# Local attention on one core: the mask band written by four small matrix tiles, and the values' copy placed between the two groups of exponentials

## The chip, the cores and the metric

The kernel runs on one core of a Trainium2 chip. The core has a matrix engine (TensorE, PE in the profile, with its weight loads shown apart as PEld), VectorE (DVE), ScalarE (ACT), GpSimd (POOL) and a queue that starts transfers (SP). Each engine runs its own list of instructions in order, and they meet only at semaphores. The time is the device time of one execution in microseconds (us); lower is better. The execution that was profiled is one execution, and its durations are those of that one.

## The reference

The input is x, 8 sequences of 512 tokens with 128 features. A first layer (clustered attention with an MLP) is computed, and then a stack of two layers with local attention. Only the local attention is touched. Cut to what matters, with 8 heads of 64 features and windows of 64 tokens:

```python
q, k, v = split(shift_token(x) @ wqkv)            # per layer, DEPTH = 2
q, k = rotary_xpos(l2norm(q) * qs, l2norm(k) * ksc)
# the keys of a window are the window before it and itself: 128 keys
sim = einsum('bhwid,bhwjd->bhwij', bq * 8, bk)
mask = (i < j) | (i > j + WINDOW) | (j == -1)     # a band; j == -1 ahead of the first window
attn = softmax(where(mask, -max, sim))
out = einsum('bhwij,bhwjd->bhwid', attn, bv)
```

So every query sees the 65 keys up to itself, which in the 64 by 128 block of a window is a diagonal band. The first window of a sequence sees only the keys of its own window.

## The kernel before

The function `local_layers` computes both layers. A tile is 128 tokens, which are two windows of 64; a layer has 32 tiles, four for each of the 8 sequences, and there are 64 tiles in all. The program is a pipeline by slots: in slot n tile T = n is projected, tile R = n - 2 is turned, tile U = n - 3 gets its scores and exponentials, and tile O = n - 4 is weighed with the values. The order on each engine is the order of the calls in that engine's `slot(n)`; no planner moves anything.

PE does in a slot, in this order: `project` of Q and K (L1360), `prob_turn` of the lower half (L1403), `scores` (L1383 and L1390), `transpose` of Q (L1372), `prob_turn` of the upper half, `project` of V, `transpose` of K, one step for a sequence that has ended, and `weigh` (L1419). That step is one of four, which go round with the tiles: the output product in two halves (L1536, two slots), the mean (L1525) and the squares (L1519). Below, a group of four slots is a round, and its slots are named output 1, output 2, mean and squares by the step that PE does in them.

`scores` first writes the mask into the scores' memory `la_s`. The tile `lw_band` holds 0 where a key is seen and -1e30 elsewhere, for 128 rows, which are the 64 queries of each of two windows; a product with a unit matrix `lw_identb` in bf16 copies it. The two products of 512 columns start the sums of two banks, `place(h)` putting the even heads in the first bank and the odd heads in the second. Then 16 f32 products add queries times keys, each in a corner of the array with 64 rows (one head of a pair) and 64 columns (one window).

There is one `la_s`. DVE takes its row maxima (`maxima`, L1603), multiplies them by the inverse norm to the bias (L1609), ACT takes the exponentials in place (`exps`, L1732, four activations for the even heads, then four for the odd ones), and in the next slot DVE divides by the sums (`share`, L1617 and L1621, by halves). The products of the next tile's band wait for both halves of `share`.

Projections and turned tiles go through two banks, `la_ring`, in turn. A product may write a bank when the one before it in that bank has been read. The bank of V is emptied by ACT in `take_values` (L1774), and the next product in that bank is the projection of Q for the next tile, which waits for `v_made`. On ACT the slot's order is: the raw copies of Q and K (L1743), their squares (L1826), the copy of half of the turned probabilities (L1749), the copy of the turned Q (L1756), `take_values`, the bias wait and the eight exponentials, and the small steps behind them (L1783, L1786, and for ended sequences L1842, L1765, L1766, L1853). SP moves the values to `la_v_back` when `v_made` is reached; they are needed four slots later by `weigh`.

DVE's slot order is: both halves of `share`, the copy out of `la_o` (L1636), four products for the rotation (L1584), maxima and bias, the other half of the turned probabilities (L1629), the copy of the turned K (L1645), norms (L1593, L1597), and one addition or subtraction of 512 columns for an ended sequence (L1713 or L1719). POOL rotates (L1883, L1889), polishes the inverse norms (L1868 to L1874), scales the keys (L1896), and once in four slots makes the shifted input of the next sequence by two copies (L1907, L1909).

Of the kernel before, what the change touches and what calls it, by code (L numbers as in the profile page):

```python
# [19 lines left out]
P = 128  # L20
B, S, D = 8, 512, 128
# [1070 lines left out]
LH, LD, WIN = 8, 64, 64  # L1092
# [15 lines left out]
def local_layers(nc, a, X, XT, C, weights):  # L1108
# [9 lines left out]
    with ExitStack() as ctx:  # L1118
# [3 lines left out]
        def ps(name, shape, dt=F32):  # L1122
            return ctx.enter_context(nc.psum_tensor(tag + name, shape, dt))

        def sem(name):
            return a["semaphores"].enter_context(nc.semaphore(tag + name))

        ident, identb, band = weights["ident"], weights["identb"], weights["band"]
# [34 lines left out]
        s_ps = ps("s", [P, LH, KEYS])  # L1163
# [25 lines left out]
        bias_made = sem("bias_made")  # L1189
        exp_half, exp_made = sem("exp_half"), sem("exp_made")  # L1190
# [29 lines left out]
        def tile_at(n):  # L1220
            for T in range(TILES):
                if slot_of(T) == n:
                    return T
            return None
# [5 lines left out]
        def ffn_at(n):  # L1230
            for f in range(BATCHES):
                if ffn_slot(f) == n:
                    return f
            return None
# [10 lines left out]
        s_flat, pT_flat = s_ps[:].rearrange("p h c -> p (h c)"), pT_ps[:].rearrange("p h c -> p (h c)")  # L1245
# [5 lines left out]
        def ring_index(T, use):  # L1251
            return 5 * (slot_of(T) + 2 * (use in (TURN_Q, TURN_K))) + use
# [7 lines left out]
        def ring_count(T, use):  # L1260

            r = ring_index(T, use)
            return sum(ring_used(x) for x in range(r + 1))
# [7 lines left out]
        def ended(n):  # L1271

            T = tile_at(n)
            return T // TPB if T is not None and T % TPB == TPB - 1 else None

        def place(h):

            return 4 * (h % 2) + h // 2
# [48 lines left out]
        def _(pe):  # L1327
# [48 lines left out]
            def scores(T):  # L1376
                b, t = T // TPB, T % TPB
                pe.wait_ge(qT_made, T + 1)
                pe.wait_ge(kT_made, T + 1)
                if T > 0:  # L1380
                    pe.wait_ge(shared, 2 * T)
                for bank in range(2):
                    nc.tensor.matmul(s_ps[:, 4 * bank:4 * bank + 4, :].rearrange("p h c -> p (h c)"), identb[:],  # L1383
                                     band[:, int(t == 0), :], start=True, stop=False, skip_group_check=True)
                for pair in range(4):
                    for w in range(2):
                        for e in range(2):
                            h = 2 * pair + e
                            key = PAD + t * P - WIN + w * WIN
                            mm = nc.tensor.matmul(s_ps[64 * w:64 * w + 64, place(h), :],  # L1390
                                                  qT[64 * e:64 * e + 64, T % 2, pair, 64 * w:64 * w + 64],
                                                  kT[64 * e:64 * e + 64, b % 2, pair, key:key + KEYS],
                                                  start=False, stop=True, skip_group_check=True)
                mm.then_inc(s_filled, 1)
# [331 lines left out]
        def _(act):  # L1726
# [3 lines left out]
            def exps(T, e):  # L1730
                for h in range(e, LH, 2):
                    ins = nc.scalar.activation(s_ps[:, place(h), :], s_ps[:, place(h), :], ACT.Exp,  # L1732
                                               bias=bias[:, T % 2, h:h + 1], scale=inv[:, T % 4, h:h + 1],
                                               accum_out=sums[:, T % 2, place(h):place(h) + 1])
                return ins
# [9 lines left out]
            def take_low(T):  # L1745
                act.wait_ge(pT_filled, 2 * T + 1)
                if T > 0:
                    act.wait_ge(o_filled, 2 * T)
                nc.scalar.activation(probT[:, 0:4], pT_ps[:, 0:4], ACT.Copy).then_inc(pT_low, 1)  # L1749

            def take_qT(T):
                r = ring_index(T, TURN_Q)
                act.wait_ge(ring_filled, ring_count(T, TURN_Q))
                if T - 1 > 0:
                    act.wait_ge(s_filled, T - 1)
                nc.scalar.activation(qT[:, T % 2].rearrange("p c q -> p (c q)"), ring_ps[:, r % 2, :],  # L1756
                                     ACT.Copy).then_inc(qT_made, 1)
# [31 lines left out]
            def take_gate(f, i):  # L1789
                j, m = NC * f + i, HC[i][1]  # L1790
                act.wait_ge(g_filled, j + 1)
                if j - 1 > 0:
                    act.wait_ge(prod_made, j - 1)
                nc.scalar.activation(gate[0:m, j % 2, :], chunk_banks(j)[0][0:m], ACT.Gelu,
                                     bias=b1[0:m, 1, i:i + 1]).then_inc(gate_made, 1)

            def take_hn(f):
                act.wait_ge(divided, f + 1)
                if f % B == 0:
                    act.wait_ge(ffn_loaded, 16 * FFN_LOADS * (f // B + 1))  # L1800
                if NC * (f - 1) > 0:
                    act.wait_ge(a_filled, NC * (f - 1))
                nc.scalar.activation(hn[:, f % 2, :], batch_at(C, f), ACT.Identity,
                                     scale=ln[:, 0:1], bias=ln[:, 1:2]).then_inc(hn_made, 1)

            def slot(n):
                T, N, R, U, O = (tile_at(n - x) for x in (0, 1, 2, 3, 4))
                f, ahead = ffn_at(n), ffn_at(n + 1)
                if f is not None:
                    if O is not None:  # L1810
                        take_low(O)
                        O = None
                    for i in range(NC):
                        take_gate(f, i)
                        if i == 0 and ahead is not None:
                            take_hn(ahead)
                if f is not None and f == B - 1:
                    nc.scalar.preload_act_table_set("natural_log_exp_and_others")
                if T is not None:
                    take_raw(T, 0)  # L1820
                    take_raw(T, 1)
                if N is not None:
                    act.wait_ge(raw_made, 2 * N + 2)
                    if N > 0:
                        act.wait_ge(sum_made, N)
                    nc.scalar.activation(squares[:], raw[:, N % 2], ACT.Square).then_inc(sq_made, 1)  # L1826
                if O is not None:
                    take_low(O)
                if R is not None:
                    take_qT(R)  # L1830
                if T is not None:
                    take_values(T)
                if U is not None:
                    act.wait_ge(bias_made, U + 1)
                    exps(U, 0).then_inc(exp_half, 1)
                    exps(U, 1).then_inc(exp_made, 1)
                b = ended(n - 6)
                if b is not None:
                    act.wait_ge(c_made, b + 1)
                    if b > 0:  # L1840
                        act.wait_ge(m_filled, m_count(b - 1, SQUARE))
                    nc.scalar.activation(csq[:], batch_at(C, b), ACT.Square).then_inc(csq_made, 1)  # L1842
                if N is not None:
                    inverse_norms(N)
                b = ended(n - 5)
                if b is not None:
                    shift(b)
                b = ended(n - 7)
                if b is not None:
                    act.wait_ge(m_filled, m_count(b, SQUARE))  # L1850
                    if b - 1 > 0:
                        act.wait_ge(dev_inverted, b - 1)
                    nc.scalar.activation(var[:, b % 2], m_ps[:, 0:TPB], ACT.Identity, bias=eps[:]  # L1853
                                         ).then_inc(var_made, 1)
                if ahead is not None and f is None:
                    take_hn(ahead)
# [93 lines left out]
def band_mask():  # L1950

    r, c = np.arange(P)[:, None] % WIN, np.arange(KEYS)[None, :]
    seen = (c >= r) & (c <= r + WIN)
    first = seen & ((np.arange(P)[:, None] >= WIN) | (c >= WIN))
    both = np.where(np.stack([seen, first], 1), 0.0, NEG).astype(np.float32)
    return np.ascontiguousarray(np.tile(both, (1, 1, 4)))

# [17 lines left out]
```

## Time and profile before

| | us |
|---|---|
| median of 3 runs | 1480.23 |
| lowest and highest run | 1479.69 to 1481.54 |
| the profiled execution | 1484.96 |
| span of that execution, first to last instruction | 1483.2 |
| granted TensorE clock, mean | 0.957 of full speed |

The local layers fill the span from about 703 us to its end. The steady part of the first layer runs from about 740 to 990 us and that of the second from about 1121 to 1387 us; between and behind them lie the feed-forward parts, which PE fills. In a timeline row the columns are start, duration, engine, line, operation, and what is written and read with shapes; `xN` stands for N merged instructions, and the bracket at the end is the idle time of the engine before the row with what ended it. Where instructions overlap in their engine's pipeline, a recorded duration is longer than the distance to the next start. In the chain of work that ended last, each row is a piece of that chain with its start and its length.

### The profile page before, as it was taken

What the parts mean: (1) busy time and instruction counts of PE and PEld (TensorE: products, weight loads), DVE (VectorE), ACT (ScalarE), POOL (GpSimd) and SP (SyncE); (2) the same over time, 40 slices, a digit from 0 to 9 for tenths busy, and PEclk for the clock granted to TensorE, in tenths of its full rate; (3) what the DMA queues carried; (4) which work ended last, traced back from release to release, by engine and by line L of the source; (5) the groups of instructions that cost most, each with busy time, mean ns of one, the idle gap of its engine ahead of it and who ended that gap; (6) DMA issues with size and microseconds to landing.
All of it is one profiled execution on the core that took longest, in us unless ns stands there. A gap on an engine that the chain in (4) does not pass through costs nothing.

```text
span 1483.2 us, 27541 instructions
## 1 busy us (share of the span) xinstructions
PE 1283.4 (87%) x9444; PEld 647.8 (44%) x9508; DVE 1096.4 (74%) x1943; ACT 1000.0 (67%) x2313; POOL 822.4 (55%) x1005
## 2 busy tenths in 40 slices
PE   3478999899998978598689999988978999999898
PEld 1112322232222212166256666665435666666654
DVE  5778888888887867123599999985448999998544
ACT  4236667666666666587488899885348898988532
POOL 3666776676666620122687788760047777887100
PEclk9569999999999999899799999999999999999899
DMA  3614333333333320100111111100101111111001
GB/s 102 114 36 77 60 65 62 75 61 62 66 71 61 62 51 1 48 10 2 39 27 27 27 30 30 27 19 12 36 22 41 27 27 30 26 27 27 1 15 43
DMA packets 161118, 60.85 MB, mean 41 GB/s; under 512 B 139690, under 2 KB 152788, under 8 KB 160980
## 3 DMA queue, kind: packets, MB, share of 16 engines
q1 hardware_dynamic: 160980, 59.09, 18.8%
q8 instruction: 77, 1.26, 0.4%
q14 instruction: 61, 0.50, 0.1%
HBM read 8.60 MB, written 2.10 MB: 7 GB/s over the span
## 4 chain that ended last, share of the span: by engine, by line
PE 29%; ACT 10%; DVE 7%; issue 4%; POOL 1%; ACTq 0%; DVEq 0%; POOLq 0%
ACT la_s L1732 8%; PE la_ring L1360 6%; PE la_s L1390 4%; PE la_ring L1372 3%; PE la_pT L1464 3%; DVE la_prob L1621 2%; PE la_pT L1403 2%; PE la_m L1536 2%; PE la_ring L1452 1%; PE la_s L1454 1%; PE la_pT L1454 1%; PE la_s L1452 1%; ACT la_v_own L1774 1%; DVE la_sumsq L1593 1%; PE la_s L1383 1%
## 5 line engine op out<-in xcount | busy, mean ns | idle before, releaser
L618 DVE TENSOR_REDUCE row_max<-max_ps 128x2 f32<-128x1024 f32 x256 | 313.0, 1223 | 70.2 <-PE max_ps L430 68.9
L670 ACT ACTIVATE prob<-scores_ps 128x1024 f32<-128x1024 f32 x256 | 262.2, 1024 | 147.5 <-PE scores_ps L410 144.0
L1732 ACT ACTIVATE la_s<-la_s,la_bias,la_inv 128x128 f32<-128x128 f32 x512 | 223.5, 442 | 8.4 <-DVE la_bias L1609 8.4
L1883 POOL TENSOR_TENSOR la_turned<-la_raw,lw_rot 128x1024 f32<-128x1024 f32 x64 | 150.9, 2358 | 127.5 <-PE la_ring L1372 83.7
L1360 PE MATMUL la_ring<-lw_wqkv,la_hT 128*128 128x512 f32 x384 | 200.6, 633 | 15.5 <-DVE la_swapped L1584 6.9
L410 PE MATMUL scores_ps<-stack 128*128 128x512 f16 x512 | 155.5, 386 | 42.0 <-ACT prob L670 41.1
L1889 POOL TENSOR_TENSOR la_turned<-la_turned,la_swapped 128x1024 f32<-128x1024 f32 x64 | 150.7, 2355 | 5.0
L444 PE MATMUL heads_ps<-prob,v_pad 128*32 128x512 f32 x1024 | 137.2, 608 | 1.1 <-ACT prob L670 1.1
L430 PE MATMUL max_ps<-stack 24*128 24x512 f16 x512 | 102.5, 397 | 31.0 <-DVE row_max L618 18.6
L410 PEld LDWEIGHTS scores_ps<-stack 128*128 128x128 f16 x512 | 34.2, 97 | 208.7 <-ACT prob L670 161.6
L1584 DVE TENSOR_TENSOR la_swapped<-la_ring,lw_rot 128x256 f32<-128x256 f32 x256 | 90.9, 416 | 32.2 <-ACT la_raw L1743 22.7
L1732 ACT ACTIVATION_READ_ACCUMULATOR la_s<-la_s,la_bias,la_inv 128x1 f32 x512 | 111.0, 217 | 0.0
L776 POOL TENSOR_TENSOR cl<-cl,cl_inv 128x512 f32<-128x512 f32 x60 | 63.0, 1050 | 85.0 <-DVE cl_inv L559 85.0
L1360 PEld LDWEIGHTS la_ring<-lw_wqkv,la_hT 128*128 128x128 f32 x384 | 64.5, 194 | 63.3 <-issue 40.0
L1621 DVE TENSOR_TENSOR la_prob<-la_s,la_inv_sum 128x512 f32<-128x512 f32 x128 | 88.5, 691 | 4.8 <-DVE la_inv_sum L1617 0.5
L1403 PE MATMUL la_pT<-mlp_ident,la_prob 128*128 128x128 f32 x512 | 79.7, 279 | 12.7 <-DVE la_prob L1621 11.0
L1372 PE MATMUL la_ring<-mlp_ident,la_turned 128*128 128x128 f32 x512 | 81.9, 283 | 8.8 <-DVE la_swapped L1584 7.8
L1603 DVE TENSOR_REDUCE la_neg_max<-la_s 128x8 f32<-128x1024 f32 x64 | 78.2, 1222 | 9.3 <-PE la_s L1390 8.2
L960 POOL TENSOR_TENSOR mlp_base<-X,Z 128x512 f32<-128x512 f32 x8 | 10.2, 1270 | 134.1 <-POOLq L257 89.4
L467 PE MATMUL bench<-w_cl,xnT 128*128 128x512 f32 x128 | 79.6, 710 | 4.6 <-ACT xnT L675 4.1
L1743 ACT ACTIVATE la_raw<-la_ring 128x512 f32<-128x512 f32 x128 | 70.6, 589 | 18.8 <-PE la_ring L1360 17.2
L1372 PEld LDWEIGHTS la_ring<-mlp_ident,la_turned 128*128 128x128 f32 x512 | 58.3, 142 | 57.2 <-ACT la_qT L1756 21.9
(177 smaller groups left out, 2741.7 us busy)
## 6 DMA issues: line engine op xcount, KB each, us to landing
la_v_back<-la_v_own SPq DMA_DIRECT2D x112, 128.0 KB, 2.3
X<-in_x SPq DMA_DIRECT2D x8, 256.0 KB, 4.8
stack<-stack_tok SPq DMA_TRANSPOSE x128, 3.2
out<-X SPq DMA_DIRECT2D x8, 256.0 KB, 2.3
lw_wqkv<-in_wqkv SPq DMA_DIRECT2D x2, 768.0 KB, 4.8
stack<-shift_row SPq DMA_DIRECT2D x64, 2.0 KB
lw_rot<-in_rot SPq DMA_DIRECT2D x2, 512.0 KB, 6.3
lw_w<-in_fw SPq DMA_DIRECT2D x2, 341.0 KB
```

The source lines that it names most:

```text
L410: mm = nc.tensor.matmul(scores_ps[:, i, :], stack[:, par, 1, h, kt * P:(kt + 1) * P], stack[:, par, 0, h, :], start=True, stop=True)
L430: mm = nc.tensor.matmul(max_ps[:, e, :], stack[rows, b % 2, 0, 2 * pair + e, qt * P:(qt + 1) * P], stack[rows, b % 2, 1, 2 * pair + e, :], ...
L444: mm = nc.tensor.matmul(heads_ps[32 * j:32 * j + 32, :], v_pad[:, par, kt, 4 * g + j, :], prob[:, c % 4, j, :], start=(kt == 0), stop=(kt ...
L618: nc.vector.tensor_reduce(row_max[:, grp % 2, w // 2, :, w % 2], max_ps[:], AX.X, ALU.max).then_inc(max_made, 1)
L670: nc.scalar.activation(prob[:, c % 4, 2 * pr:2 * pr + 2, :], scores_ps[:], ACT.Exp, scale=1.0 / LOGIT_SCALE).then_inc(exp_made, 1)
L1360: mm = nc.tensor.matmul(ring_ps[:, r % 2, :], hT[:, b % 2, t * P:(t + 1) * P], wqkv[:, at:at + INNER], start=True, stop=True)
L1372: mm = nc.tensor.transpose(ring_ps[:, r % 2, c * P:(c + 1) * P], turned[:, T % 2, SIDE[use], c * P:(c + 1) * P], ident[:])
L1403: mm = nc.tensor.transpose(pT_ps[:, j, :], prob[:, T % 2, j, :], ident[:])
L1621: nc.vector.tensor_tensor(prob[:, T % 2, heads], s_ps[:, heads], inv_sum[:, heads].unsqueeze(2).to_broadcast([P, 4, KEYS]), ALU.mult).then ...
L1732: ins = nc.scalar.activation(s_ps[:, place(h), :], s_ps[:, place(h), :], ACT.Exp, bias=bias[:, T % 2, h:h + 1], scale=inv[:, T % 4, h:h + ...
L1883: nc.gpsimd.tensor_tensor(spun, raw[:, T % 2].rearrange("p s (h f) -> p s h f", f=LD), rot[:, T % TPB, :, 0, :].unsqueeze(2).to_broadcast( ...
L1889: nc.gpsimd.tensor_tensor(turned[:, T % 2], turned[:, T % 2], swapped[:], ALU.add).then_inc(added_rot, 1)
```

## The change

The change edits `scores`, the order of three calls on ACT, and the table of the mask.

- Two products of a 128 by 128 unit matrix with 512 columns become four, each of a 64 by 64 unit matrix with 512 columns. Each stands in its own corner of the array: row half e and bank e (even or odd heads), column half w (the window). They use the corners in the order in which the 16 products behind them do.
- Both halves of rows of `lw_band` are now read for one window alone, so the table for the first window of a sequence masks the keys ahead of it in all rows, and it is used where t == 0 and w == 0.
- On ACT the copy of the values stands between the first four exponentials and the last four, and the wait for the bias stands ahead of the first four.

```diff
-                for bank in range(2):
-                    nc.tensor.matmul(s_ps[:, 4 * bank:4 * bank + 4, :].rearrange("p h c -> p (h c)"), identb[:],
-                                     band[:, int(t == 0), :], start=True, stop=False, skip_group_check=True)
+                for w in range(2):
+                    for e in range(2):
+                        rows = slice(64 * e, 64 * e + 64)
+                        nc.tensor.matmul(s_flat[64 * w:64 * w + 64, e * S:(e + 1) * S], identb[rows, rows],
+                                         band[rows, int(t == 0 and w == 0), :],
+                                         start=True, stop=False, skip_group_check=True)
...
+                if U is not None:
+                    act.wait_ge(bias_made, U + 1)
+                    exps(U, 0).then_inc(exp_half, 1)
                 if T is not None:
                     take_values(T)
                 if U is not None:
-                    act.wait_ge(bias_made, U + 1)
-                    exps(U, 0).then_inc(exp_half, 1)
                     exps(U, 1).then_inc(exp_made, 1)
...
-    first = seen & ((np.arange(P)[:, None] >= WIN) | (c >= WIN))
+    first = seen & (c >= WIN)
```

PE in a slot of the steady part, from the projections of Q and K to the scores; before:

```order
L1360 MATMUL la_ring<-lw_wqkv,la_hT 128x512 [waits la_v_made]
L1360 MATMUL la_ring<-lw_wqkv,la_hT 128x512 [waits la_kT_made]
L1403 MATMUL la_pT<-mlp_ident,la_prob 128x128 [waits la_pT_low,la_shared]
L1403 MATMUL la_pT<-mlp_ident,la_prob 128x128 x3
L1383 MATMUL la_s<-lw_band,lw_identb 128x512 [waits la_shared,la_kT_made,la_qT_made]
L1383 MATMUL la_s<-lw_band,lw_identb 128x512
L1390 MATMUL la_s<-la_kT,la_qT 64x128 x16
```

and after:

```order
L1360 MATMUL la_ring<-lw_wqkv,la_hT 128x512 [waits la_v_made]
L1360 MATMUL la_ring<-lw_wqkv,la_hT 128x512 [waits la_kT_made]
L1406 MATMUL la_pT<-mlp_ident,la_prob 128x128 [waits la_pT_low,la_shared]
L1406 MATMUL la_pT<-mlp_ident,la_prob 128x128 x3
L1385 MATMUL la_s<-lw_band,lw_identb 64x512 [waits la_shared,la_kT_made,la_qT_made]
L1385 MATMUL la_s<-lw_band,lw_identb 64x512 x3
L1393 MATMUL la_s<-la_kT,la_qT 64x128 x16
```

Nothing on PE changed its place; two wide products became four small ones with the same waits on the first, and the shape of PE's tiles now changes ahead of the band and no longer behind it.

ACT in a slot of the steady part, from the copy of the turned Q to the exponentials' end; before:

```order
L1756 ACTIVATE la_qT<-la_ring 128x512 [waits la_s_filled,la_ring_filled]
L1774 ACTIVATE la_v_own<-la_ring 128x512 [waits la_o_filled,la_ring_filled]
L1732 ACTIVATE la_s,la_sums<-la_s,la_bias,la_inv 128x128 [waits la_bias_made]
L1732 ACTIVATE la_s,la_sums<-la_s,la_bias,la_inv 128x128 x7
L1783 ACTIVATE la_lnsq<-la_sumsq 128x16 [waits la_scaled,la_exp_made,la_clip_made]
```

and after:

```order
L1759 ACTIVATE la_qT<-la_ring 128x512 [waits la_s_filled,la_ring_filled]
L1735 ACTIVATE la_s,la_sums<-la_s,la_bias,la_inv 128x128 [waits la_bias_made]
L1735 ACTIVATE la_s,la_sums<-la_s,la_bias,la_inv 128x128 x3
L1777 ACTIVATE la_v_own<-la_ring 128x512 [waits la_o_filled,la_ring_filled]
L1735 ACTIVATE la_s,la_sums<-la_s,la_bias,la_inv 128x128 x4
L1786 ACTIVATE la_lnsq<-la_sumsq 128x16 [waits la_scaled,la_exp_made,la_clip_made]
```

The copy of the values (`la_v_own`) moved behind four exponentials, and what ACT waits for behind the copy of the turned Q is now the bias, no longer the projection of V. DVE, POOL and SP keep their lists.

## Rows read from the trace of the kernel before

**Rows 1.** The page: busy time of each engine over the span.

```profile
PE 1283.4 (87%) x9444; PEld 647.8 (44%) x9508; DVE 1096.4 (74%) x1943; ACT 1000.0 (67%) x2313; POOL 822.4 (55%) x1005
```

**Rows 2.** Windows, one round: busy time (x instructions) by engine, then clock.

```profile
core 0: us, PE busy (x) PEld busy (x) DVE busy (x) ACT busy (x) POOL busy (x), PEclk, DMA share, GB/s
866.48:902.25 35.77, 34.09 (x375) 23.18 (x378) 33.17 (x63) 32.20 (x102) 28.57 (x31) 1.00 0.12 27
```

**Rows 3.** Timeline of PE: the band in one round and in the next.

```profile
866.48 0.38 PE L1383 MATMUL la_s<-lw_band,lw_identb 128*128 128x512 bf16 x1 [0.46 <-DVE la_prob L1621]
...
875.23 0.38 PE L1383 MATMUL la_s<-lw_band,lw_identb 128*128 128x512 bf16 x1 [0.80 <-DVE la_prob L1621]
...
884.18 0.38 PE L1383 MATMUL la_s<-lw_band,lw_identb 128*128 128x512 bf16 x1
...
893.13 0.38 PE L1383 MATMUL la_s<-lw_band,lw_identb 128*128 128x512 bf16 x1
...
902.25 0.38 PE L1383 MATMUL la_s<-lw_band,lw_identb 128*128 128x512 bf16 x1 [0.46 <-DVE la_prob L1621]
```

**Rows 4.** Timeline of PEld and PE: loads of band and scores, squares slot.

```profile
866.24 0.13 PEld L1383 LDWEIGHTS la_s<-lw_band,lw_identb 128*128 128x128 bf16 x2 [0.45 <-issue]
866.79 0.86 PEld L1390 LDWEIGHTS la_s<-la_kT,la_qT 64*64 64x64 f32 x32 [0.42 <-issue]
...
866.79 1.10 PE L1390 MATMUL la_s<-la_kT,la_qT 64*64 64x128 f32 x32
867.82 0.66 PE L1372 MATMUL la_ring<-mlp_ident,la_turned 128*128 128x128 f32 x4
```

**Rows 5.** Chain that ended last: squares slot, values' copy to the next band.

```profile
869.82 0.60 ACT la_v_own L1774
...
873.97 0.19 DVE la_inv_sum L1617
...
874.18 0.70 DVE la_prob L1621
874.88 0.35 issue
```

**Rows 6.** Timeline of ACT: copies of values in squares, output 2 and mean slots.

```profile
870.31 0.43 ACT L1732 ACTIVATE la_s<-la_s,la_bias,la_inv 128x128 f32<-128x128 f32 x1
...
887.51 0.60 ACT L1774 ACTIVATE la_v_own<-la_ring 128x512 f32<-128x512 f32 x1 [0.70 <-PE la_ring L1360]
...
896.71 0.60 ACT L1774 ACTIVATE la_v_own<-la_ring 128x512 f32<-128x512 f32 x1 [0.29 <-PE la_ring L1360]
```

**Rows 7.** Timeline of DVE: rotation and maxima (squares), bias in three slots.

```profile
866.64 1.41 DVE L1584 TENSOR_TENSOR la_swapped<-la_ring,lw_rot 128x256 f32<-128x256 f32 x4
867.96 1.23 DVE L1603 TENSOR_REDUCE la_neg_max<-la_s 128x8 f32<-128x1024 f32 x1
869.22 0.59 DVE L1609 TENSOR_TENSOR la_bias<-la_neg_max,la_inv 128x8 f32<-128x8 f32 x1
...
886.92 0.17 DVE L1609 TENSOR_TENSOR la_bias<-la_neg_max,la_inv 128x8 f32<-128x8 f32 x1
...
896.49 0.17 DVE L1609 TENSOR_TENSOR la_bias<-la_neg_max,la_inv 128x8 f32<-128x8 f32 x1
```

**Rows 8.** Timeline of POOL in the squares slot: the second input copy.

```profile
869.18 0.61 POOL L1909 COPY la_hT<-XT 64x511 f32<-64x511 f32 x1
```

**Rows 9.** Timeline of ACT, DVE and PE in the mean slot.

```profile
893.28 1.08 ACT L1743 ACTIVATE la_raw<-la_ring 128x512 f32<-128x512 f32 x2
...
893.91 1.42 DVE L1584 TENSOR_TENSOR la_swapped<-la_ring,lw_rot 128x256 f32<-128x256 f32 x4 [0.64 <-ACT la_raw L1743]
...
894.72 0.66 PE L1372 MATMUL la_ring<-mlp_ident,la_turned 128*128 128x128 f32 x4 [0.18 <-DVE la_swapped L1584]
...
899.00 1.98 PE L1360 MATMUL la_ring<-lw_wqkv,la_hT 128*128 128x512 f32 x4
901.13 0.66 PE L1403 MATMUL la_pT<-mlp_ident,la_prob 128*128 128x128 f32 x4
```

## The prediction

> **What bounds the kernel now.** I read the page first, for its shares: PE is busy for 87% of the span, and no engine is near full [rows 1]. A busy share says little here, because all engines pass work to each other in a ring. So the second view is the windows, cut to one round of four slots in the steady part: in 35.77 us PE has 34.09 us of work, DVE 33.17, ACT 32.20, POOL 28.57, at the full 2.4 GHz level of the clock [rows 2]. Three engines lie within 2 us of each other; what one of them saves is worth only what the next one leaves. The third view is therefore PE's timeline at one place, the band, since its products must wait for `share` of the tile before [rows 3]. The four slots take 875.23 - 866.48 = 8.75 us (squares), 8.95 (output 1), 8.95 (output 2) and 9.12 (mean). The bracket tells what ends each. Behind the squares slot PE had waited 0.80 us for DVE's `la_prob`, behind the mean slot 0.46 us; behind both output slots it had not waited at all. So two slots are bound by PE's own list, and two by a loop over DVE, ACT and PE. The reader should expect different gains in them, and the sum is made slot by slot.
>
> The loop of the squares slot stands in the chain that ended last [rows 5]: values' copy at 869.82, eight exponentials from 870.31 [rows 6], then `la_inv_sum` at 873.97, `la_prob` until 874.88, 0.35 us to PE's recorded band product.
>
> **Part 1, the band.** Of the two products only the second has a record; both weight loads are there. From the first load (866.24) to the scores' first load (866.79) the band takes 0.55 us [rows 4]. The recorded second product starts 0.24 us after the first load [rows 3, 4], so a stream of 512 columns takes at most 0.24 us, and what is left of the 0.55 behind two streams, about 0.1 us, is the change from one wide tile to four small ones. The change asks for four streams in four corners. How far they overlap no row shows for bf16 and 512 columns. The nearest row is that of the scores, which use the same four corners in the same order: 32 records start within 867.82 - 866.79 = 1.03 us, one per 32 ns, while a record stays on for far longer [rows 4]. If the band starts in that rhythm, the four start within 0.1 us, the first corner is free after 0.24 us, and the scores follow corner by corner: 0.24 us as seen by the scores. That is the lower bound. The upper bound is no overlap, 4 x 0.24 = 0.96 us. I take 0.24, since the scores are the same corners on the same data path. The 0.1 us of the tile change stays, and stands now ahead of the band. So 0.55 becomes 0.34: **0.21 us less of PE in a slot where PE does not wait**, and 0.31 less behind a wait, because the tile change can be done during it.
>
> In the two output slots all of it counts: 2 x 0.21 = 0.42 us. There `share` has some slack, since PE came to the band without a wait.
>
> In the squares slot the earlier scores find DVE busy. It ends `share`, copies `la_oT`, rotates from 866.64 on, and the maxima begin at 867.96, as soon as the rotation's row lets them [rows 7], with the scores over at about 867.89. So a band that is 0.3 us shorter gives 0.07 us at most there; what is late next is DVE's own list.
>
> **Part 2, the values' copy.** Three costs are to be weighed. ACT waits 0.70 us for the projection of V in the output 2 slot, and copies at 887.51; the bias has been ready since 886.92 + 0.17 = 887.09 [rows 6, 7]. With the new order the exponentials begin 0.42 us earlier, and the copy of 0.5 us stands in the middle with its wait gone. The total of ACT's work is the same; 0.42 us of idle time leaves. In an output slot PE is the bound, so this buys nothing there by itself. But it is inherited: behind output 2 ACT makes the two shifted copies and only then the raw copy at 893.28; DVE had waited 0.64 us for it and PE 0.18 us for DVE [rows 9]. With 0.42 us less ahead of them PE's 0.18 us go. **The mean slot gains 0.18 + 0.21 = 0.39 us**, since from its band to the turned K it is PE's list, and what follows on DVE begins with that. Its last part (norms, subtraction, both halves of `share`) keeps its length.
>
> In the squares slot the bias was not ready at 869.39 as 0.17 us would have it: it took 0.59 us and ended at 869.81 [rows 7], at the moment when POOL ended its second copy for the next sequence's input, 869.18 + 0.61 = 869.79 [rows 8]. The values' copy began at 869.82 [rows 5]. So here the bias is no earlier than the values, the exponentials start at about 869.83, the copy adds its 870.31 - 869.82 = 0.49 us in their middle, and they end when they did. **The squares slot gains 0.0 us.** The Trainium skill, "SBUF — State Buffer", section "SBUF: two separate sides", has a rule for this: a DVE operation with two inputs in SBUF and a GpSimd operation that reads it exclude each other for the whole instruction. The trace agrees with it at this place, by the 0.59 us against 0.17 in the other slots; by a reading without the rule this slot would gain as well, and the time would be that of rival A.
>
> What is queued behind the moved copy: four exponentials and all of ACT's slot behind them, which is no later than before. Who waits for it is the next projection of Q on PE and the transfer on SP. The copy now ends half of 873.97 - 870.31 [rows 5, 6] and 0.5 us, about 2.3 us, after the exponentials' start, at 872.2 in the squares slot, where PE came to that projection at 872.0; 0.2 us that the 0.80 us of wait ahead of the band take in [rows 3]. In the output slots it ends near 889.5, well ahead of 890.66, when PE is through with its list. In the mean slot it ends near 899.0 at the latest while PE comes at 899.00 - 0.39 [rows 9]; behind it PE waited at 901.13 for the probabilities, so up to 0.3 us are covered. The transfer feeds a product four slots later and has some 35 us. Part 2 alone therefore costs nothing in my sum, and its cover is the wait behind each of those two slots.
>
> **The sum.** Per round 0.21 + 0.21 + 0.39 + 0.0 = 0.81 us of 35.77. There are 64 tiles, so 16 rounds; the first and last tiles of a layer lack the steps of ended sequences and wait longer ahead of the band, but they have the same two edits, and I give them the same. 16 x 0.81 = 13.0 us. The profiled execution, 1484.96 us around a span of 1483.2, would become about 1472.0 around 1470.2. It lies 0.3% above the median of the runs, so the gain is taken from the median: 1480.23 - 13.0 = **1467.2 us**. The feed-forward parts and the first layer are not touched.
>
> **Rivals.**
> A. The squares slot gains too, because POOL's two copies come off the bias when everything shifts. The slot would lose up to the 0.42 us of the held bias, less what the next limit leaves, say 0.3: 16 x 0.3 = 4.8 us more, 1462.4 us. Against it: those copies follow the turned K at a fixed distance, and DVE's chain does as well. Chance 0.14.
> B. The small products overlap only in pairs, by column half or by their loads, and the band costs what it did. Only the mean slot's 0.18 us and some idle time at the layers' ends remain, 16 x 0.18 = 2.9 plus up to 2, about 4.5 us: 1475.7 us. For it: the scores are f32 products of 128 columns, and no row shows bf16 streams of 512 columns in four corners. The Trainium skill, "TensorE: Matmul & The Clock Gate", section on LDWEIGHTS, gives a load the number of its columns over 1.2 in ns, so four loads of 64 columns would take 213 ns by it, an estimate; if they lay bare, the gain of part 1 would be nil as in B. The scores' rhythm of 32 ns speaks against loads that lie bare [rows 4]. Chance 0.14.
> C. The values' copy holds PE's projection of Q in the mean slot by the whole 0.4 us, and that gives back its gain: 16 x 0.39 = 6.2 less, 1473.4 us. Chance 0.09.
> D. Slower: the four products run one after another, as they would if two products that end in the same columns' outputs could not pass each other. The band is then 0.96 + 0.1 instead of 0.55, at least 0.4 us more in each slot that PE binds: 0.4 + 0.4 + (0.4 - 0.18) = 1.02 per round, the squares slot hides it under the rotation and the held bias; 16 x 1.02 = 16.3, 1496.5 us. It decides from the point where four streams take more than about 0.5 us together. The scores' rhythm speaks against it. Chance 0.05.
> E. Nothing measurable: B and C together. About 1479 us, chance 0.06.
>
> **How the numbers follow.** The forecast has 0.52, with a range of its own from 1463 to 1471 for the unknown size of the band (0.15 to 0.35 us). The range for 8 in 10 reaches from just below A to just above B, 1461 to 1476, and leaves out D, E and the outer parts of A and B. About 0.2% (3 us) is what a measurement of this kernel can tell from no change. Faster by more than that: forecast, A, B, C less a little, 0.87. Within it: 0.08. Slower: 0.05.
>
> **What would show it.** After the change the distance from the band's first load to the scores' first load should be near 0.25 us; if it is over 0.5, D or B holds. The two output slots should take 8.74 us each, still without a wait ahead of the band; the mean slot 8.73, its wait for `la_swapped` gone; the squares slot still 8.75 with a bias near 0.6 us. A shorter bias there and a slot near 8.45 mean A. A wait of the projection of Q for `la_v_own` that is followed by a later band means C. I would be wrong as a whole if the clock of the steady part fell from its level, or if DVE, with 33.17 us a round, has waits that I take for slack.

## The result and the profile after

| | before | after |
|---|---|---|
| median, us | 1480.30 (4 runs) | 1466.05 (4 runs) |
| lowest and highest run | 1479.69 to 1481.54 | 1464.31 to 1467.65 |
| ratio after / before, 95% interval | | 0.9897 (0.9882 to 0.9913) |
| profiled execution, us | 1484.96 | 1465.55 |
| its span, us | 1483.2 | 1463.7 |

The forecast was 1467.2 us; the kernel takes 1466.05, 14.3 us less than before. That is 1.0% of the whole, and the interval, 12.9 to 17.5 us less, leaves no doubt about the sign. In the session of three of the experiments below, one execution of `e3_band_twice` (1699.17 us at a granted clock of 0.738) and one of the kernel before (1505.41 us at 0.911) ran slow, and they are left out of its times and ratios.

The two profiled spans differ by 19.5 us, more than the medians do. The chain of work that ended last says where, in each. The first of the long feed-forward pieces `la_pT` starts at 1029.73 before and 1022.38 after, 7.35 us earlier; that is the first layer. The same piece of the second layer starts 19.4 us earlier. The windows around the end of the second layer's attention show why that layer seems worth more (columns as in [rows 2]). Before:

```profile
1378.80:1391.00 12.20, 10.01 (x127) 7.65 (x128) 7.77 (x14) 6.66 (x24) 1.24 (x2) 0.84 0.01 1
1391.00:1405.00 14.00, 12.41 (x98) 9.20 (x99) 4.97 (x9) 6.96 (x20) 1.02 (x1) 0.65 0.00 1
```

After:

```profile
1360.00:1372.00 12.00, 9.06 (x138) 6.67 (x140) 9.90 (x19) 10.27 (x38) 1.92 (x5) 1.00 0.01 1
1372.00:1386.00 14.00, 11.39 (x145) 8.37 (x137) 7.07 (x13) 7.97 (x23) 1.02 (x1) 1.00 0.01 1
```

The granted clock was 0.65 over 14 us in the profiled execution of before and 1.00 after. In that execution PE stood at its lower level (1.2 GHz) for a while, behind 12.2 us in which it had had 10.01 us of work. From the last band (1386.68 before, 1371.65 after) to the feed-forward piece it took 26.6 us against 22.2. I count those 4.4 us as no gain of the change: they are about what the profiled execution of before lies above its median (4.7 us). The same happened the other way behind the first layer: from its last band (1007.40 before, 998.52 after) to the feed-forward piece it took 22.3 us before and 23.9 after, at a granted clock of 1.00 and 0.96 from 991 to 1030 us. What the slots gained is therefore best read from the first band of a layer to its last: 277.07 us before and 269.04 after in the first layer, 277.43 and 269.87 in the second, 8.03 + 7.56 = 15.6 us in all.

A round in the steady part of the profile after, on PE's timeline, to be laid beside [rows 3]:

```profile
862.42 0.41 PE L1385 MATMUL la_s<-lw_band,lw_identb 64*64 64x512 bf16 x4 [0.25 <-DVE la_prob L1624]
...
871.19 0.41 PE L1385 MATMUL la_s<-lw_band,lw_identb 64*64 64x512 bf16 x4 [0.37 <-DVE la_prob L1624]
...
879.88 0.41 PE L1385 MATMUL la_s<-lw_band,lw_identb 64*64 64x512 bf16 x4
...
888.58 0.41 PE L1385 MATMUL la_s<-lw_band,lw_identb 64*64 64x512 bf16 x4
...
897.20 0.41 PE L1385 MATMUL la_s<-lw_band,lw_identb 64*64 64x512 bf16 x4 [0.24 <-DVE la_prob L1624]
```

The window of that round, beside [rows 2]:

```profile
862.42:897.20 34.78, 33.55 (x386) 23.12 (x387) 32.65 (x63) 32.01 (x101) 28.49 (x32) 1.00 0.12 28
```

The round fell from 35.77 to 34.78 us, by 0.99. Slot by slot, from band to band:

| us | squares | output 1 | output 2 | mean | round |
|---|---|---|---|---|---|
| before | 8.75 | 8.95 | 8.95 | 9.12 | 35.77 |
| forecast | 8.75 | 8.74 | 8.74 | 8.73 | 34.96 |
| after | 8.77 | 8.69 | 8.70 | 8.62 | 34.78 |

All four slots are where the forecast put them within 0.11 us, and the output slots still have no wait ahead of the band. The squares slot gained nothing. On ACT, before, it was the projection of V that ended the wait in this slot:

```profile
869.82 0.60 ACT L1774 ACTIVATE la_v_own<-la_ring 128x512 f32<-128x512 f32 x1 [0.70 <-PE la_ring L1360]
```

After, it is the bias:

```profile
865.99 0.43 ACT L1735 ACTIVATE la_s<-la_s,la_bias,la_inv 128x128 f32<-128x128 f32 x1 [0.95 <-DVE la_bias L1612]
...
867.74 0.60 ACT L1777 ACTIVATE la_v_own<-la_ring 128x512 f32<-128x512 f32 x1
```

DVE took 0.60 us for that bias and ended it with POOL's second input copy. Then PE, which had waited for nothing at this place before, waits for the values' copy:

```profile
865.36 0.60 DVE L1612 TENSOR_TENSOR la_bias<-la_neg_max,la_inv 128x8 f32<-128x8 f32 x1
...
865.33 0.61 POOL L1913 COPY la_hT<-XT 64x511 f32<-64x511 f32 x1
...
868.40 1.98 PE L1360 MATMUL la_ring<-lw_wqkv,la_hT 128*128 128x512 f32 x4 [0.51 <-ACT la_v_own L1777]
```

865.36 + 0.60 = 865.96 and 865.33 + 0.61 = 865.94. ACT waits 0.95 us for the bias, and the values' copy, 0.5 us of ACT's time, now stands behind four exponentials and no longer in front of them. This became the question of the experiments: the sum had come out, but did each part do what its term says?

### The profile page after: what moved, and what is told of

Its sections match the earlier page's. It is cut to its first block, busy times and chain, and to the rows that moved or that the text cites. A ratio compares the mean times of both kernels' runs of the same rounds, so it can differ in the third digit from the quotient of the medians.

```text
span 1463.7 us, 27861 instructions
## 1 busy us (share of the span) xinstructions
PE 1270.5 (87%) x9636; PEld 643.8 (44%) x9636; DVE 1090.6 (75%) x1943; ACT 997.8 (68%) x2313; POOL 821.0 (56%) x1005
## 3 DMA queue, kind: packets, MB, share of 16 engines
q8 instruction: 78, 1.28, 0.4%
## 4 chain that ended last, share of the span: by engine, by line
PE 24%; DVE 13%; ACT 9%; issue 4%; POOL 2%; DVEq 0%; ACTq 0%; POOLq 0%
ACT la_s L1735 7%; PE la_ring L1360 5%; DVE la_neg_max L1606 3%; DVE la_swapped L1587 3%; PE la_pT L1467 3%; DVE la_prob L1624 2%; PE la_m L1539 2%; PE la_ring L1372 2%; PE la_s L1393 2%; PE la_ring L1455 1%; PE la_s L1457 1%; PE la_pT L1457 1%; PE la_s L1455 1%; PE la_o L1422 1%; PE la_pT L1406 1%
## 5 line engine op out<-in xcount | busy, mean ns | idle before, releaser
L767 POOL TENSOR_TENSOR cl_half<-cl 128x256 f32<-128x256 f32 x60 | 44.0, 733 | 68.7 <-ACT cl L703 68.7
```

## The experiments

Two theories. **Theory 1** is the forecast's: the parts add up, the band with 0.2 to 0.26 us in three slots, the order in the mean slot alone, and the squares slot is fixed by the bias. **Theory 2**: the parts overlap. In the squares slot the bias is late, the old order does the values' copy in that wait, and the new order takes it out of there; so the order gives in the mean slot and takes in the squares slot.

### One part at a time

`e1_band_only` has the four small products and the old order on ACT:

```diff
                 if R is not None:
                     take_qT(R)
+                if T is not None:
+                    take_values(T)
                 if U is not None:
                     act.wait_ge(bias_made, U + 1)
                     exps(U, 0).then_inc(exp_half, 1)
-                if T is not None:
-                    take_values(T)
-                if U is not None:
                     exps(U, 1).then_inc(exp_made, 1)
```

> Only the band of the change (four small tiles); the values' copy stands ahead of all eight exponentials, as before. Theory 1 (the parts add up as predicted, and the held bias fixes the squares slot): the band gives 0.26 us in the three other slots of a round, the squares slot stays at 8.75 us: 16 x 0.78 = 12.5, about 1468 us. Theory 2 (the parts overlap: in the squares slot the copy of 0.5 us fits into ACT's wait for the late bias, and the new order takes it out of that wait): the squares slot falls to about 8.45 us, the mean slot keeps most of its old length (its wait for the raw copy stays, gain 0.1 us): 16 x (0.26 + 0.26 + 0.1 + 0.3) = 14.7, about 1465.6 us, no slower than the whole change.

`e2_order_only` has the new order (the same lines the other way round, put into the kernel before) and the two wide products.

> Only the order of the change (values' copy between the two groups of exponentials); the band is the two wide products of before. Theory 1: the mean slot loses its 0.18 us wait of PE and nothing else moves: 16 x 0.2 = 3 us, 1477 us. Theory 2: the mean slot gains about 0.3, the squares slot nothing or loses a little: 16 x 0.3 = 5 us, 1475.3 us. By both, the band is worth more than the order, and the output slots stay at 8.95 us.

Beside them, on the same chip, ran the change itself.

> The changed kernel itself, beside the three others on the same chip, so that they can be compared with it: about 14 us faster than the kernel before, 1466 us, by either theory.

| | median, us | ratio to before, interval |
|---|---|---|
| band only | 1465.87 (1463.96 to 1467.75) | 0.9890 (0.9873 to 0.9907) |
| order only | 1476.37 (1473.57 to 1478.99) | 0.9961 (0.9946 to 0.9976) |
| both, the change | 1466.50 (1466.33 to 1468.24) | 0.9898 (0.9879 to 0.9917) |

Before had 1481.92 in that session. Band alone is worth 16.1 us, order alone 5.5, both together 15.4. On top of the small band the new order is worth nothing that these times can show. The times do not decide between the theories: `e1_band_only` lies at Theory 2's 1465.6, but one of its four runs (1467.75) is at Theory 1's 1468, and `e2_order_only` lies between 1477 and 1475.3. The slots decide. Theory 1 asked for 8.75 us in the squares slot, and this is `e1_band_only` from the squares slot on:

```profile
862.47 0.41 PE L1385 MATMUL la_s<-lw_band,lw_identb 64*64 64x512 bf16 x4 [0.24 <-DVE la_prob L1624]
...
870.87 0.41 PE L1385 MATMUL la_s<-lw_band,lw_identb 64*64 64x512 bf16 x4 [0.58 <-DVE la_prob L1624]
...
879.56 0.41 PE L1385 MATMUL la_s<-lw_band,lw_identb 64*64 64x512 bf16 x4
...
888.26 0.41 PE L1385 MATMUL la_s<-lw_band,lw_identb 64*64 64x512 bf16 x4
...
897.28 0.41 PE L1385 MATMUL la_s<-lw_band,lw_identb 64*64 64x512 bf16 x4 [0.24 <-DVE la_prob L1624]
```

Squares 8.40, output 8.69 and 8.70, mean 9.02, round 34.81. Against the change (8.77, 8.69, 8.70, 8.62) the squares slot is 0.37 us shorter and the mean slot 0.40 us longer. The new order moved 0.4 us from one slot to the other. The timeline of ACT in the squares slot of `e1_band_only`, with DVE's bias beside it, shows how:

```profile
865.67 0.60 ACT L1777 ACTIVATE la_v_own<-la_ring 128x512 f32<-128x512 f32 x1 [0.55 <-PE la_ring L1360]
866.16 0.42 ACT L1735 ACTIVATE la_s<-la_s,la_bias,la_inv 128x128 f32<-128x128 f32 x1
...
865.41 0.60 DVE L1612 TENSOR_TENSOR la_bias<-la_neg_max,la_inv 128x8 f32<-128x8 f32 x1
```

The bias is as late as in the change (866.01), but the copy is done while ACT waits for it, and the exponentials follow 0.15 us after the bias with nothing to interrupt them. Theory 2 holds. From the band's first weight load to the bias's end it is 3.57 us before, 3.58 with the band alone and 3.57 in the change; from the same load to the start of the values' copy it was 3.58 us before and is 3.24 with the band alone.

The mean slot is 9.02 us here, 0.10 less than before, and PE waits in it for DVE's rotation longer than before (0.18 us, [rows 9]):

```profile
889.96 0.66 PE L1372 MATMUL la_ring<-mlp_ident,la_turned 128*128 128x128 f32 x4 [0.42 <-DVE la_swapped L1587]
```

`e2_order_only` has 8.76 us in the squares slot, 8.95 in both output slots and 8.85 in the mean slot: on the wide band the new order gives 0.27 us in the mean slot and takes no more than 0.01 in the squares slot. Its PE timeline has both records of the wide band; the output 2 slot:

```profile
878.93 0.60 PE L1403 MATMUL la_pT<-mlp_ident,la_prob 128*128 128x128 f32 x4
879.37 0.59 PE L1383 MATMUL la_s<-lw_band,lw_identb 128*128 128x512 bf16 x2
879.89 1.10 PE L1390 MATMUL la_s<-la_kT,la_qT 64*64 64x128 f32 x32
880.93 0.66 PE L1372 MATMUL la_ring<-mlp_ident,la_turned 128*128 128x128 f32 x4
```

and the same slot in the change:

```profile
879.35 0.60 PE L1406 MATMUL la_pT<-mlp_ident,la_prob 128*128 128x128 f32 x4
879.88 0.41 PE L1385 MATMUL la_s<-lw_band,lw_identb 64*64 64x512 bf16 x4
880.12 1.04 PE L1393 MATMUL la_s<-la_kT,la_qT 64*64 64x128 f32 x32
881.10 0.66 PE L1372 MATMUL la_ring<-mlp_ident,la_turned 128*128 128x128 f32 x4
```

Both slots are bound by PE. The wide band holds the scores for 879.89 - 879.37 = 0.52 us, the small one for 0.24. The change of tile shape now stands ahead of the band, where the distance from `la_pT` to it grew by 0.09 us (0.53 against 0.44). And the scores themselves take 0.98 us against 1.04; that this is because they no longer begin with the change of shape is likely, but no run shows it. In sum 1.75 against 2.00 us: 0.25.

### The band's streams

`e3_band_twice` issues the four small products twice. What that adds is the cost of four streams without the change of tile shape.

```diff
-                for w in range(2):
+                for w in (0, 1, 0, 1):
```

> The whole change, with the four small band products issued twice (the second set writes the same values over the first, so the result is the same). If four streams of 512 columns in four corners overlap fully, the second set costs one stream, 0.21 to 0.24 us, in the three slots of a round that PE binds, and the 0.37 us wait of the squares slot takes it in: 16 x 0.7 = 11 us more than the change, 1477 us. If they overlapped only in pairs, the second set would cost 0.45 us: 16 x 3 x 0.45 = 22 us more, 1488 us. If the band's low price came from something else than overlap, 0.9 us a set, 1509 us.

Measured 1472.68 us (1471.03 to 1473.46), ratio 0.9928 (0.9909 to 0.9947); the change was at 0.9898, so the second set costs about 4 to 7 us, less than the 11 expected by full overlap, and far less than the 22 or 43 of the other cases. The size is read from the timeline, output 2 slot:

```profile
882.54 0.63 PE L1385 MATMUL la_s<-lw_band,lw_identb 64*64 64x512 bf16 x8
882.99 1.04 PE L1393 MATMUL la_s<-la_kT,la_qT 64*64 64x128 f32 x32
```

Eight streams hold the scores for 0.45 us, four for 0.24: the second four cost 0.21 us, one stream. They overlap fully, and rival D and the streams' half of rival B are out. The output slots are 8.91 us each (+0.21) and the squares slot 8.77 as in the change. The mean slot, where I had expected the whole 0.21 too, is 8.73 (+0.11), so a round is 35.3 us.

### The held bias

`e4_input_copies_earlier` is the change with POOL's two input copies one slot earlier, where they meet another bias or none.

```diff
-                if T is not None and T % TPB == 1 and T % NT + 3 < NT:
-                    shift_tokens((T + 3) // TPB)
+                if T is not None and T % TPB == 0 and T % NT + 4 < NT:
+                    shift_tokens((T + 4) // TPB)
```

> The whole change, with POOL's two copies for the next sequence's input made one slot earlier (T % 4 == 0 in place of 1), so that they no longer run while DVE makes the bias of the squares slot. Theory of the held bias: the bias of the squares slot falls from 0.60 to about 0.17 us, ACT starts its exponentials 0.4 us earlier, and the slot falls from 8.77 to about 8.45 us; the copies may now touch the bias of the mean slot by 0.1 us. 16 x 0.25 = 4 us less than the change, 1462 us. Rival (the long bias comes from a wait on the inverse norms or from DVE itself): bias and slot stay, 1466 us.

1460.62 us (1460.45 to 1461.07), ratio 0.9849 (0.9834 to 0.9864). DVE's bias of the mean slot and of the squares slot, and POOL's second copy, in `e4_input_copies_earlier`:

```profile
856.22 0.25 DVE L1612 TENSOR_TENSOR la_bias<-la_neg_max,la_inv 128x8 f32<-128x8 f32 x1
864.74 0.17 DVE L1612 TENSOR_TENSOR la_bias<-la_neg_max,la_inv 128x8 f32<-128x8 f32 x1
...
855.84 0.61 POOL L1913 COPY la_hT<-XT 64x511 f32<-64x511 f32 x1
```

The squares slot's bias takes 0.17 us in place of 0.60, and the bias that the copies now touch takes 0.25 and ends with them (856.47 against 856.45). The squares slot is 8.34 us, the mean slot 8.66. The long bias was the copies' doing, and taking it away is worth 0.4 us a round. With it the wait of PE's next loads for the values' copy in the squares slot fell from 0.65 to 0.21 us.

`e5_values_first_in_squares` leaves the copies and puts the values first in one slot of four.

```diff
+                values_first = T is not None and T % TPB == 2
+                if values_first:
+                    take_values(T)
                 if U is not None:
                     act.wait_ge(bias_made, U + 1)
                     exps(U, 0).then_inc(exp_half, 1)
-                if T is not None:
+                if T is not None and not values_first:
                     take_values(T)
```

> The whole change, but in the squares slot alone (one in four) the values' copy stands ahead of the exponentials again. Theory 1: the exponentials of that slot end at the same time in either order, so the time is that of the change, 1466 us. Theory 2: in that slot ACT waits 0.95 us for a bias that POOL's copies hold, and the values' copy of 0.5 us fits into that wait; the slot falls from 8.77 to about 8.45 us: 16 x 0.3 = 4.8 us less, 1461.3 us, and PE's wait of 0.5 us for the values' copy in that slot is gone.

1461.70 us (1460.82 to 1463.46), ratio 0.9863 (0.9847 to 0.9879), beside 1466.50 for the change on the same chip. The band starts of `e5_values_first_in_squares` at both ends of the squares slot:

```profile
860.84 0.41 PE L1385 MATMUL la_s<-lw_band,lw_identb 64*64 64x512 bf16 x4 [0.24 <-DVE la_prob L1624]
...
869.24 0.41 PE L1385 MATMUL la_s<-lw_band,lw_identb 64*64 64x512 bf16 x4 [0.57 <-DVE la_prob L1624]
```

8.40 us, with the mean slot at 8.64: this takes the better slot of each order. PE's next projection of Q follows `weigh` with no wait.

`e6_both` has both edits.

> Both edits: POOL's copies one slot earlier and the values' copy first in the squares slot. If the held bias is the one cause of the squares slot's loss, the two remedies don't add up: either brings the slot to about 8.4 us, where PE's way to the projection of V, and then DVE's own list, bound it. Expected 1461.5 us, within 1 us of the better of the two. Rival (they are separate costs): 16 x 0.6 = 10 us less than the change, 1456 us.

1462.23 us (1459.47 to 1463.88), ratio 0.9855 (0.9839 to 0.9872), a round of 34.47 us with 8.41 in the squares slot. By medians that is 1.6 us above the better of the two, more than the 1 us expected, though the ranges overlap; by the slots the values' copy ahead of an early bias costs 0.07 us (8.41 against 8.34). The two remedies do not add up; they cure one loss. `e4_input_copies_earlier` beats the kernel before by 1.5% and the change by 0.5%, and `e5_values_first_in_squares` does nearly as well.

| slots, us | squares | output 1 | output 2 | mean | round |
|---|---|---|---|---|---|
| before | 8.75 | 8.95 | 8.95 | 9.12 | 35.77 |
| order only | 8.76 | 8.95 | 8.95 | 8.85 | 35.51 |
| band only | 8.40 | 8.69 | 8.70 | 9.02 | 34.81 |
| the change | 8.77 | 8.69 | 8.70 | 8.62 | 34.78 |
| band twice | 8.77 | 8.91 | 8.91 | 8.73 | 35.3 |
| values first in squares | 8.40 | 8.69 | 8.70 | 8.64 | 34.43 |
| input copies earlier | 8.34 | 8.70 | 8.69 | 8.66 | 34.39 |
| both remedies | 8.41 | 8.69 | 8.70 | 8.67 | 34.47 |

## Why the prediction was right

**The slots and their limits.** Reading the round as four slots with different ends was the step that carried. The two output slots, which PE bound, gained what PE's list lost, 0.25 us each; the two others did not follow that list alone.

**The band.** Sized at 0.21 us where PE binds, measured 0.25: 0.28 less from the band's start to the scores (0.52 to 0.24), 0.09 more ahead of the band for the change of tile shape, which only moved, and 0.06 by which the scores themselves became shorter, a term that I had not seen. The value taken from the scores' rhythm, 0.24 us for the whole band, was exact. The Trainium skill, "TensorE: Matmul & The Clock Gate", section on LDWEIGHTS, gives a load of 64 columns 53 ns, and four of them 213 ns, an estimate. Nothing of that size was added here: four loads and four streams together hold the scores for 0.24 us, and eight and eight for 0.45, so the loads lie under the streams.

**The mean slot.** 0.39 us forecast, 0.50 measured, and the two terms, 0.18 for the wait and 0.21 for the band, did not stand side by side as I had them. The order alone gives 0.27 us here and the band alone 0.10, since without the new order the band's gain goes into a longer wait for the rotation (0.42 us). With both, PE waits less than before but still a little: from the scores' start to the turned Q it is 1.08 us (888.82 to 889.90), against 0.98 in the output 2 slot and 1.28 in the mean slot of before (893.44 to 894.72). In the change:

```profile
888.82 1.04 PE L1393 MATMUL la_s<-la_kT,la_qT 64*64 64x128 f32 x32
889.90 0.66 PE L1372 MATMUL la_ring<-mlp_ident,la_turned 128*128 128x128 f32 x4
```

So ACT's raw copy and DVE's rotation, and no longer PE's list, set the start of this slot, which is why doubling the band added only 0.11 us to it. And the 0.09 us for the change of tile shape falls here into PE's wait for `la_prob` at the slot's end; I had written 0.31 us for a band behind a wait, and then put 0.21 into the sum. In three of the six such slots of the second layer's steady part the change takes 8.88 to 8.92 us, in two of them with a wait of 0.3 us for the rotation; before, one of the six is as much longer than the rest. Why is open.

**The squares slot.** 0.0 forecast, -0.02 measured, and yet this is the step with the fault. I wrote that the band would give 0.07 us at most there because DVE's own list came next, and that the order costs nothing. The experiments separate the two: the band alone gives 0.35 us in that slot (8.75 to 8.40), the new order takes 0.37 back. What I missed was that the projection of V lies behind the band on PE's list. A shorter band brings V, hence the values' copy, 0.34 us forward (3.58 to 3.24 us behind the band's first load), while the bias stays where it was (3.57 and 3.58), and the exponentials begin when both are there. Under the old order the copy hides in the wait for the bias. Under the new one that wait stands idle, 0.95 us, and the copy is paid in the middle. The held bias itself I had read rightly. The Trainium skill, "SBUF — State Buffer", section "SBUF: two separate sides", says that such an operation is blocked for the whole of a GpSimd one that reads SBUF and started first. The trace agrees: the copy started 0.03 us ahead (865.33 and 865.36) and the bias took 0.60 us; without the copies it took 0.17, and where it started 0.38 us into the copy (856.22 and 855.84) it ended with it.

**The cover of the moved copy.** I expected PE to wait 0.2 us for it in the squares slot, covered by the 0.80 us ahead of the band. It waited 0.51, since the shorter band brought PE there earlier, and 0.37 of the cover was left. So it cost nothing here, as forecast. I had read the cover as too large: in the 0.80 us lie about 0.24 in which the first wide product ran, which has no record there (its load stands at 874.99, the recorded product at 875.23). Rival C did not come true: in the mean slot the loads of that projection waited 0.17 us for the copy, and the slot gained 0.50.

**The sum.** 13.0 us forecast; the slots of the profiled executions gained 15.6, and the medians say 14.3 (12.9 to 17.5). The forecast was low by 0.04 to 0.05 us in each output slot and 0.11 in the mean slot, and the zero of the squares slot came out by two errors that cancelled, which is luck. Taking the first and last tiles of a layer like the others was right in sum and not one by one: the last four slots of each layer gained 1.51 us together (33.39 to 31.88), the first three nothing in the first layer (28.64 to 28.78) and 0.31 in the second (29.19 to 28.88).

## What to carry to other kernels

Where three engines are each busy for 90 to 95% of a round in a pipeline, cut one period of the trace into its slots, find for each what ends its wait, and price an edit slot by slot; the page's shares would have given none of these numbers. An edit of order that takes a wait from one slot can take useful work out of another slot's wait: ask of each slot whether the thing moved was hidden there, and let the order differ from slot to slot. And price two edits also one without the other, since a sum that comes out right can hold two terms that are wrong in opposite ways: the band's 0.35 us in the squares slot, and the -0.37 us of the order on top of it, were both put at zero here.

## What the runs showed of the hardware

At the full clock, four bf16 products of 512 columns in the four 64 by 64 corners of the array hold what follows for 0.24 us, and a second four add 0.21 us; two wide ones hold it for 0.52 us with the change of shape behind them. Changing from wide tiles to corner tiles took 0.09 us of PE ahead of the band, and about 0.1 us behind the wide one (0.52 - 2 x 0.21, an estimate). A DVE operation of 8 columns with both inputs in SBUF took 0.17 us alone and up to 0.60 us beside POOL's copy, and in the three cases read (before, the change, `e4_input_copies_earlier`) it ended within 0.02 us of the copy's end.
